# A fused audio-tower kernel: the factors of heads 2 to 7 get a PSUM bank of their own

## The chip, the core and the metric

The kernel runs on one core of one Trainium2 chip. A core has a matrix engine (TensorE, PE in the profile, with its weight loads as PEld), a vector engine (VectorE, DVE), an activation engine (ScalarE, ACT), a general engine (GpSimd, POOL) and queues that issue transfers (SP). Matmuls write to PSUM, which has eight banks of 2 KiB per partition; a 375-column float32 result takes one. The metric is the device time of one launch in microseconds; lower is better.

## What is computed

Sixteen sequences of 750 x 64 pass a token mixer (four 64 x 64 layers, a strided convolution to 375 positions), a retention layer, a product-key memory with attention over it, an inner gradient step of a two-layer network, and a mixture of experts. Nearly all the time is in the product-key memory:

```python
sim = jnp.einsum('pbnhd,pkhd->pbnhk', q, pk_keys)          # two halves, 64 keys each
scores, idx = jax.lax.top_k(sim, 16)                       # of each half
score = scores[0][..., :, None] + scores[1][..., None, :]  # 256 candidates
final_scores, pk_idx = jax.lax.top_k(score, 16)            # 16 of 4096 rows
final_scores = jax.nn.softmax(final_scores, axis=-1)
k = jnp.einsum('bnhk,bnhkd->bnhd', final_scores, keys_table[ind])
v = jnp.einsum('bnhk,bnhkd->bnhd', final_scores, values_table[ind])
```

The kernel doesn't gather the 16 rows. For each head and position it builds the dense row of 4096 weights, which is zero but at the 16 picks, and multiplies it with the whole table of 4096 x 128 (keys and values side by side).

## The kernel before

**Steps and slots.** A sequence has 8 heads, a head has 32 chunks of 128 table rows, so there are 256 steps per sequence. Step j makes the weights of one chunk in a bank of `dense` and sums them into `accu`. The work is spread over slots: in slot j PE runs the `spread` matmul of step j-2 (L506), the `accu` matmul of step j-6 (L520, float32), and the `hot` matmul of step j (L528). ACT reads the bank of step j-2 into `dense_w` (L904, counted by the semaphore `taken`), then applies a steep ramp in place to the bank of step j (L910, `past`). POOL multiplies `dense_w` by the first factor (L449, `weighed`). `hot` of step j may start when its bank is free.

**Factors.** The steps of a head read four factors (k = 0 to 3) that DVE has made in rows (`ranks`, `firsts`, `seconds`). PE turns each by three matmuls into PSUM (k=0 at L492, k=1 in float32 at L494, k=2 and 3 at L496), and ACT copies it into `store` (L890, L892, L894, counted by `factor_kept`). The factors of head 0 come ahead of slot 0, those of head 1 in slots 0, 2, 4 and 6, the 24 of heads 2 to 7 in every second slot from 30 to 76.

**The ring.** Steps and factors take the three banks of `dense` in turn, in the order of `ORDER.items`. So the n-th item waits for the reader of item n-3. Without a factor between, that is step j-3; with one among the last three, it is step j-2, whose `taken` is ACT's work of the same slot.

**What lies between the slots.** Each engine's program is in a fixed, hand-written order. While the slots of sequence b run, the other layers run in between, in pieces: `prepare(b + 1)` (mixer, convolution, layer norm, retention) with `FILL_PREPARE` slots between its pieces (slots 19 to 51), `similarities(b + 1, 0)`, `gradient(b - 1)` with `FILL_GRADIENT` slots between (52 to 81), and later the attention of b. In slots 28 to 82 the pieces on PE are, in order: turning the first norm (L467), the projections (L580, L581), the retention scores (L586, L588), the retention mix (L595), turning the second norm (L467), the similarities (L611), and in the gradient L710, L716, L720, L723, L729 and L736. DVE works on the same chain: the norms (L1147), the rotation (L1197), the decay (L1202), the silu products (L1380 to L1397), and between them it makes the rows of the factors, with a comparison (L1294) and a reduction (L1299) for each pair of heads.

**The two banks `sims`.** The projections and the retention use both; the similarities use both and are copied out by ACT (L956); the gradient uses only the second, `sims[:, 1]`; the attention's scores use both.

## Time and profile before

| | |
|---|---|
| time, median of 3 runs | 6420.99 us (6412.18 to 6425.69) |
| the profiled execution | 6410.07 us, span 6408.2 us |
| PE busy | 5616.6 us, 88% of the span |
| ACT busy | 4644.2 us, 72% |
| DVE busy | 4242.5 us, 66% |
| POOL busy | 4212.2 us, 66% |
| PE's granted clock, mean | 0.974 of full |

The profile shows one execution. A row of a timeline gives start, duration, engine, line and operation, and in brackets the idle time of the engine ahead of it with what ended it. Instructions of one engine overlap in the records (a matmul's record of 0.33 us is followed by the next start 0.16 us later), so the distance between starts tells what an instruction costs, not its duration. The 16 sequences follow each other about 370 us apart. The timelines below are of sequence 5 (the sixth) where nothing else is said.

### The profile page before, as it was taken

To read this page: it belongs to the slowest core of one execution; us is meant where nothing else is said; L and a number is where in the kernel's file an instruction comes from. 1 tells how busy PE (TensorE), PEld (TensorE's weight loads), DVE (VectorE), ACT (ScalarE), POOL (GpSimd) and SP (SyncE) were. 2 spreads that over 40 slices of the span, in tenths; PEclk is the share of its full clock that TensorE was granted. 3 is DMA by queue.
4 is the path that set the end of the run, shared out by engine and by line. 5 is a ranking of instruction groups with operands and counts; after the bars stand their busy time and mean duration, and the time that the engine had idled before them with its cause. 6 is when DMAs were issued, how large, how long until landed. Compare 5 with 4: busy or idle time off the path is not lost.

```text
span 6408.2 us, 79708 instructions
## 1 busy us (share of the span) xinstructions
PE 5616.6 (88%) x24704; PEld 3125.1 (49%) x24704; DVE 4242.5 (66%) x13138; ACT 4644.2 (72%) x10889; POOL 4212.2 (66%) x4108
## 2 busy tenths in 40 slices
PE   2599998989989898989989898899989899999977
PEld 1345454545545454454545455454545545454533
DVE  7676766848585784858568484957758485772157
ACT  1577777878777786877778787777778777777833
POOL 0386766858586685958677585867768585777700
PEclk9999999999999999999999999999999999999968
DMA  1111111111111111111111111111111111111100
GB/s 35 37 56 41 50 48 41 56 37 56 42 50 46 47 52 37 56 39 53 46 47 52 40 53 39 53 46 47 52 37 58 38 53 43 49 48 50 45 21 15
DMA packets 93462, 290.42 MB, mean 45 GB/s; under 512 B 17880, under 2 KB 26547, under 8 KB 92781
## 3 DMA queue, kind: packets, MB, share of 16 engines
q1 hardware_dynamic: 92748, 285.25, 13.5%
q8 instruction: 197, 3.23, 0.2%
q14 instruction: 229, 1.87, 0.1%
q10 hardware_dynamic: 288, 0.07, 0.0%
HBM read 280.68 MB, written 4.61 MB: 45 GB/s over the span
## 4 chain that ended last, share of the span: by engine, by line
PE 60%; POOL 16%; ACT 16%; DVE 6%; issue 2%; DMA 0%; SPq 0%; DVEq 0%; ACTq 0%
PE accu L520 26%; POOL dense_w L449 16%; PE dense L528 9%; PE dense L506 7%; ACT dense L910 4%; ACT dense_w L904 3%; PE sims L641 3%; PE work L647 2%; PE work L568 1%; PE work L685 1%; PE dense L494 1%; PE dense L816 1%; PE work L634 1%; PE work L621 1%; PE sims L611 1%
## 5 line engine op out<-in xcount | busy, mean ns | idle before, releaser
L449 POOL TENSOR_TENSOR dense_w<-dense_w,store 128x375 f32<-128x375 f32 x4096 | 4209.8, 1049 | 1868.2 <-ACT dense_w L904 1825.2
L520 PE MATMUL accu<-dense_w,store 128*128 128x375 f32 x8192 | 3321.8, 488 | 182.4 <-POOL dense_w L449 123.4
L910 ACT ACTIVATE dense<-dense 128x375 f32<-128x375 f32 x4096 | 1917.1, 468 | 782.5 <-PE dense L528 540.1
L904 ACT ACTIVATE dense_w<-dense 128x375 f32<-128x375 f32 x4096 | 1962.4, 479 | 218.1 <-PE dense L506 216.5
L520 PEld LDWEIGHTS accu<-dense_w,store 128*128 128x128 f32 x8192 | 1434.8, 194 | 496.1 <-POOL dense_w L449 172.0
L528 PE MATMUL dense<-store,hot 128*128 128x375 bf16 x4096 | 1337.8, 327 | 250.1 <-ACT dense_w L904 248.6
L506 PE MATMUL dense<-store,spread 96*128 96x375 bf16 x4096 | 1348.5, 329 | 13.7 <-ACT dense L910 11.0
L528 PEld LDWEIGHTS dense<-store,hot 128*128 128x128 bf16 x4096 | 394.8, 97 | 1114.6 <-ACT dense_w L904 703.3
L1299 DVE TENSOR_REDUCE store<-picks 125x256 bf16<-125x4096 uint16 x192 | 848.6, 4420 | 6.6
L506 PEld LDWEIGHTS dense<-store,spread 96*128 96x128 bf16 x4096 | 402.1, 98 | 793.8 <-ACT dense L910 560.2
L1294 DVE TENSOR_TENSOR picks<-codes,keys 125x4096 uint16<-125x4096 uint16 x192 | 527.7, 2749 | 7.3 <-ACTq L897 1.9
L1340 DVE TENSOR_TENSOR shared<-sims,mask 125x750 f32<-125x750 f32 x64 | 59.9, 936 | 407.5 <-PE sims L641 407.5
L1361 DVE TENSOR_TENSOR h<-h_now,work 125x192 f32<-125x192 f32 x16 | 5.7, 354 | 303.7 <-PE work L694 303.7
L647 PE MATMUL work<-shared 125*64 125x375 f32 (+2 forms) x768 | 195.8, 391 | 10.4 <-ACT shared L1010 10.4
L1340 DVE TENSOR_TENSOR prob_odd<-sims,mask 125x750 f32<-125x750 f32 x64 | 59.9, 936 | 198.4 <-PE sims L641 198.4
L641 PE MATMUL sims<-kvT,qT 128*125 128x125 f32 (+2 forms) x768 | 184.7, 376 | 0.2 <-ACT kvT L915 0.2
L1247 DVE TENSOR_TENSOR cand<-s 125x16 f32<-125x16 f32 (+5 forms) x384 | 181.4, 541 | 1.1
L1231 DVE FIND_INDEX8 i<-s,front 125x8 uint32<-125x64 f32 x768 | 165.4, 215 | 0.0
L1232 DVE MATCH_REPLACE8 front<-s,front 125x64 f32<-125x64 f32 x768 | 158.0, 206 | 0.0
L1221 DVE MAX8 s<-front 125x8 f32<-125x64 f32 x768 | 101.9, 210 | 84.5 <-ACT front L956 83.9
L1242 DVE FIND_INDEX8 i<-s,front 125x8 uint32<-125x64 f32 x768 | 150.2, 217 | 0.0
L1380 DVE SCALAR_TENSOR_TENSOR shared<-work,mb_s,shared 64x375 f32<-64x375 f32 x16 | 9.6, 600 | 202.5 <-ACT shared L1036 202.5
(255 smaller groups left out, 6048.1 us busy)
## 6 DMA issues: line engine op xcount, KB each, us to landing
store<-in SPq DMA_DIRECT2D x513, 512.0 KB, 3.3
x_in<-in SPq DMA_DIRECT2D x16, 187.5 KB, 2.4
store<-in SPq DMA_DIRECT2D x1, 2048.0 KB, 8.7
queries_kept<-n3T SPq DMA_DIRECT2D x16, 93.8 KB, 3.4
h_saved<-h SPq DMA_DIRECT2D x16, 93.8 KB
store<-queries_kept SPq DMA_DIRECT2D x16, 93.8 KB, 2.4
store<-h_saved SPq DMA_DIRECT2D x16, 93.8 KB
out<-store SPq DMA_DIRECT2D x16, 93.8 KB
```

Of the source, the lines that this page charges most:

```text
L449: nc.gpsimd.tensor_tensor(dense_w[:, i % RING, :], dense_w[:, i % RING, :], first_of[:, i // CHUNKS, :], ALU.mult).then_inc(s["weighed"], 1)
L506: mm(dense[:, ORDER.step[i] % BANKS, 0:S], spread[0:3 * I1S, c % (CHUNKS // GROUPS), :], second_of[0:3 * I1S, c // (CHUNKS // GROUPS), h, ...
L520: last = mm(accu[:, 0, 0:S], table[:, n % PIECE_RING, i % PIECE, :], dense_w[:, i % RING, :], start=(c == 0), stop=(c == CHUNKS - 1))
L528: mm(to[:, 0:S], hot[:, j % CHUNKS, :], ranksT[:, j // CHUNKS, :], start=True, stop=True, skip_group_check=True).then_inc(s["coded"], 1)
L641: last = mm(dst, qT[:, h % 2, tile(i)], kvT[:, h, 0:(i + 1) * P], start=True, stop=True)
L647: last = mm(work[D:128, 0, j * P:S], vo[:, j, h * D:(h + 1) * D], pT[:, min(j, 1), (0, 0, 2 * P)[j]:(S, 2 * P, S)[j]], start=(h == 0 and j ...
L904: fn(dense_w[:, i % RING, :], dense[:, ORDER.step[i] % BANKS, 0:S], ACT.Relu, scale=-1.0).then_inc(s["taken"], 1)
L910: fn(here, here, ACT.Relu, scale=FAR).then_inc(s["past"], 1)
L1231: v.max_index(i16[:, g, 0:8], s16[:, g, 0:8], rest[:, g, :])
L1247: v.tensor_tensor(cand[:, :, off:off + m], s16[:, H:, 0:m], s16[:, 0:H, a:a + 1].broadcast_to([P, H, m]), ALU.add)
L1294: v.tensor_tensor(hit, codes[:, h:h + 2].unsqueeze(3).broadcast_to([P, 2, 2, SUB, K]), keys[:].unsqueeze(1).unsqueeze(1).broadcast_to([P, ...
L1299: v.tensor_reduce(ranks[:, t, h:h + 2, :].rearrange("p h (a i) -> p h a i", a=2), hit, AX_X, ALU.min).then_inc(s["pick_step"], 1)
```

## The change

The factors of heads 0 and 1 stay in the ring. Those of heads 2 to 7 are written to `sims[:, 0]` and read from there by ACT. Their slots are now 30, 32, 34, 36 (ahead of the projections, which need `sims`), then 46, 48, 50 (after the retention), then every second slot from 52 to 84: none stands any more in slots 38 to 44, and four stand in 78 to 84. A factor waits until ACT has kept the one before it. PE waits for the kept factors (`sims_free`) ahead of the projections and ahead of each of the three similarities. `wait_ge(sim_kept)` after the first similarities now stands for the second sequence too.

```diff
+PREPARE_AT = EARLY
+ROTATE_AT = PREPARE_AT + sum(FILL_PREPARE[:6])
+MIXED_AT = PREPARE_AT + sum(FILL_PREPARE[:8])
+GRADIENT_AT = PREPARE_AT + sum(FILL_PREPARE)
+OWN_BANK = 2
+LATER_SLOTS = [*range(ROTATE_AT - 8, ROTATE_AT, 2), *range(MIXED_AT, GRADIENT_AT, 2)]
+LATER_SLOTS += [GRADIENT_AT + 2 * n for n in range((H - OWN_BANK) * FACTORS - len(LATER_SLOTS))]
...
-            if self.factor_at(j) is not None:
+            if self.factor_at(j) is not None and self.factor_at(j)[0] < OWN_BANK:
                 items.append(("factor", self.factor_at(j)))
...
-                to = bank_free(b, ORDER.factor[h, k])
+                if h < OWN_BANK:
+                    to = bank_free(b, ORDER.factor[h, k])
+                else:
+                    pe.wait_ge(s["factor_kept"], (b * H + h) * FACTORS + k)
+                    to = sims[:, 0]
...
                 pe.wait_ge(s["nT_done"], b * 2 + 1)
+                sims_free(b, ROTATE_AT)
...
+            def sims_free(b, j):
+                if b >= 1:
+                    turned_so_far = OWN_BANK * FACTORS + sum(at < j for at in LATER_SLOTS)
+                    pe.wait_ge(s["factor_kept"], (b - 1) * H * FACTORS + turned_so_far)
+
             def similarities(b, t):
 
+                sims_free(b, GRADIENT_AT if t == 0 else SLOTS)
...
-                n = ORDER.factor[h, k]
                 act.wait_ge(s["factored"], (b * H + h) * FACTORS + k + 1)
-                src = dense[:, n % BANKS, 0:S]
+                src = (dense[:, ORDER.factor[h, k] % BANKS] if h < OWN_BANK else sims[:, 0])[:, 0:S]
```

Three places of PE's order follow, each with before first and the change second. Lines of the changed kernel are 13 to 20 higher (L506 is L519, L520 is L533, L528 is L541, L494 is L507, L496 is L509, L492 is L505).

First place: slots 34 to 35, after the first norm is turned. Before:

```order
L467 MATMUL work<-ident,nrm 64x125 [waits ln_n]
L467 MATMUL work<-ident,nrm 64x125 x2
L506 MATMUL dense<-store,spread 128x375 [waits past]
L496 MATMUL dense<-ident_b,store 96x125 [waits factor_kept]
L496 MATMUL dense<-ident_b,store 96x125 x2
L520 MATMUL accu<-dense_w,store 128x375 [waits weighed]
L528 MATMUL dense<-store,hot 128x375 [waits taken]
```

After:

```order
L476 MATMUL work<-ident,nrm 64x125 [waits ln_n]
L476 MATMUL work<-ident,nrm 64x125 x2
L519 MATMUL dense<-store,spread 128x375 [waits past]
L509 MATMUL sims<-ident_b,store 96x125 [waits factor_kept]
L509 MATMUL sims<-ident_b,store 96x125 x2
L533 MATMUL accu<-dense_w,store 128x375 [waits weighed]
L541 MATMUL dense<-store,hot 128x375 [waits taken]
```

The instructions and their order are the same; the factor writes `sims`, and the `taken` that the last row waits for is that of step 31 now (j-3) and was that of step 32 (j-2).

Second place: slots 38 and 39, after the projections. Before:

```order
L581 MATMUL sims<-halves,wrope_s 64x375
L506 MATMUL dense<-store,spread 128x375 [waits past]
L492 MATMUL dense<-ident_b,store 128x125 [waits factor_kept]
L492 MATMUL dense<-ident_b,store 128x125 x2
L520 MATMUL accu<-dense_w,store 128x375 [waits weighed,acc_done,piece_in0]
L528 MATMUL dense<-store,hot 128x375 [waits taken]
L506 MATMUL dense<-store,spread 128x375 [waits past]
L520 MATMUL accu<-dense_w,store 128x375 [waits weighed]
L528 MATMUL dense<-store,hot 128x375 [waits taken]
```

After:

```order
L595 MATMUL sims<-halves,wrope_s 64x375
L519 MATMUL dense<-store,spread 128x375 [waits past]
L533 MATMUL accu<-dense_w,store 128x375 [waits weighed,acc_done,piece_in0]
L541 MATMUL dense<-store,hot 128x375 [waits taken]
L519 MATMUL dense<-store,spread 128x375 [waits past]
L533 MATMUL accu<-dense_w,store 128x375 [waits weighed]
L541 MATMUL dense<-store,hot 128x375 [waits taken]
```

The factor is gone from here, as from slots 40, 42 and 44.

Third place: slots 77 and 78, after the gradient's last matmuls. Before:

```order
L736 MATMUL work<-dzt,xt 65x64 x5
L506 MATMUL dense<-store,spread 128x375 [waits past]
L520 MATMUL accu<-dense_w,store 128x375 [waits weighed]
L528 MATMUL dense<-store,hot 128x375 [waits taken]
L506 MATMUL dense<-store,spread 128x375 [waits past]
L520 MATMUL accu<-dense_w,store 128x375 [waits weighed,piece_in1]
L528 MATMUL dense<-store,hot 128x375 [waits factor_kept]
```

After:

```order
L756 MATMUL work<-dzt,xt 65x64 x5
L519 MATMUL dense<-store,spread 128x375 [waits past]
L533 MATMUL accu<-dense_w,store 128x375 [waits weighed]
L541 MATMUL dense<-store,hot 128x375 [waits taken]
L519 MATMUL dense<-store,spread 128x375 [waits past]
L505 MATMUL sims<-ident_b,store 128x125 [waits factor_kept]
L505 MATMUL sims<-ident_b,store 128x125 x2
L533 MATMUL accu<-dense_w,store 128x375 [waits weighed,piece_in1]
L541 MATMUL dense<-store,hot 128x375 [waits taken]
```

The first factor of head 7 stands here now; the other three follow in slots 80, 82 and 84.

## Rows read from the trace of the kernel before

**Rows 1.** The page: the group of `hot` matmuls with its idle time.

```profile
L528 PE MATMUL dense<-store,hot 128*128 128x375 bf16 x4096 | 1337.8, 327 | 250.1 <-ACT dense_w L904 248.6
```

**Rows 2.** Windows, `hot` matmuls alone: steps with factors (sequence 15), without.

```profile
5793.12:5815.07 21.95, 5.29 (x16) 1.52 (x17) 1.00 0.16 51
2251.61:2259.23 7.62, 2.57 (x8) 0.77 (x8) 1.00 0.21 67
```

**Rows 3.** Timeline of PE, slots 63 to 65, the first with a float32 factor.

```profile
2161.70 0.83 PE L494 MATMUL dense<-ident,store 125*128 125x125 f32 x6
2162.37 0.80 PE L520 MATMUL accu<-dense_w,store 128*128 128x375 f32 x2
2163.00 0.32 PE L528 MATMUL dense<-store,hot 128*128 128x375 bf16 x1
...
2164.27 0.33 PE L528 MATMUL dense<-store,hot 128*128 128x375 bf16 x1 [0.15 <-ACT dense_w L904]
...
2164.61 0.33 PE L496 MATMUL dense<-ident_b,store 125*96 125x125 bf16 x3
2164.77 0.85 PE L520 MATMUL accu<-dense_w,store 128*128 128x375 f32 x2
```

**Rows 4.** Timeline of ACT in the same slots.

```profile
2163.36 0.47 ACT L910 ACTIVATE dense<-dense 128x375 f32<-128x375 f32 x1 [0.32 <-PE dense L528]
2163.74 0.48 ACT L904 ACTIVATE dense_w<-dense 128x375 f32<-128x375 f32 x1
```

**Rows 5.** Timeline of PE, the pieces between the slots, slots 28 to 77.

```profile
2095.82 1.44 PE L568 MATMUL work<-tapdiag,mixed 128*125 128x64 f32 x11
2106.15 0.48 PE L467 MATMUL work<-ident,nrm 125*64 125x125 f32 x3
2111.74 0.84 PE L580 MATMUL work<-halves,wrope_s 64*64 64x375 f32 x2
2126.44 1.42 PE L595 MATMUL work<-v_s,shared 125*125 125x64 f32 x12
2135.82 0.48 PE L467 MATMUL work<-ident,nrm 125*64 125x125 f32 x3
2150.13 0.84 PE L716 MATMUL work<-x,params 64*64 64x375 f32 x2
2158.21 0.84 PE L720 MATMUL sims<-x,params 64*64 64x375 f32 x2
2168.54 0.84 PE L723 MATMUL work<-halves,w1T_s 64*64 64x375 f32 x2
2182.42 0.75 PE L736 MATMUL work<-dzt,xt 125*65 125x64 f32 x10
```

**Rows 6.** Timeline of DVE: the ends of the chains that PE waits for.

```profile
2102.89 1.32 DVE L1147 TENSOR_SCALAR nrm<-h,mv,rstd 125x64 f32<-125x64 f32 x3
2125.60 0.28 DVE L1202 TENSOR_TENSOR shared<-sims,decay 125x125 f32<-125x125 f32 x1
2159.69 0.60 DVE L1380 SCALAR_TENSOR_TENSOR shared<-sims,mb_s,shared 64x375 f32<-64x375 f32 x1 [0.84 <-ACT shared L1036]
2167.27 1.22 DVE L1397 TENSOR_TENSOR halves<-shared 64x375 f32<-64x375 f32 x1
```

**Rows 7.** Windows, all engines: slots 28 to 76 of sequence 5.

```profile
2097.26:2182.42 85.16, 74.51 (x359) 38.24 (x358) 41.38 (x141) 61.86 (x142) 49.32 (x49) 1.00 0.12 38
```

**Rows 8.** Timeline of POOL while DVE runs L1294 (slots 38 to 41).

```profile
2116.72 5.11 POOL L449 TENSOR_TENSOR dense_w<-dense_w,store 128x375 f32<-128x375 f32 x3 [0.41 <-ACT dense_w L904]
```

**Rows 9.** Timeline of PE after L716, sequences 5 and 6; then a window of 6.

```profile
2154.10 0.33 PE L528 MATMUL dense<-store,hot 128*128 128x375 bf16 x1 [2.00 <-ACT dense_w L904]
...
2526.86 0.33 PE L528 MATMUL dense<-store,hot 128*128 128x375 bf16 x1 [2.01 <-ACT dense_w L904]
...
2532.18 0.84 PE L720 MATMUL sims<-x,params 64*64 64x375 f32 x2
...
2526.00:2532.20 6.20, 5.19 (x17) 2.63 (x17) 5.02 (x5) 4.08 (x10) 4.20 (x4) 0.72 0.00 0
```

More of the change, by code:

```diff
@@ L37 @@
 FACTORS = 4
-PREPARED_EVERY, LATER_FROM = 2, 30
+PREPARED_EVERY = 2
 PIECE = 8
@@ L66 @@
 assert sum(PICKS_INSIDE) == PIECES_SOON
+PREPARE_AT = EARLY
[5 more added lines that the diff above has]
+LATER_SLOTS += [GRADIENT_AT + 2 * n for n in range((H - OWN_BANK) * FACTORS - len(LATER_SLOTS))]
+assert LATER_SLOTS[-1] < GRADIENT_AT + sum(FILL_GRADIENT) + FILL_FIRST[0]
 class Schedule:
@@ L86, in factor_at @@
     def factor_at(j):
-        if j >= LATER_FROM:
-            j -= LATER_FROM - FACTORS * PREPARED_EVERY
-        elif j >= FACTORS * PREPARED_EVERY:
-            return None
-        n, odd = divmod(j, PREPARED_EVERY)
-        n += FACTORS
-        return divmod(n, FACTORS) if odd == 0 and n < H * FACTORS else None
+        if j < FACTORS * PREPARED_EVERY:
+            n, odd = divmod(j, PREPARED_EVERY)
+            return (1, n) if odd == 0 else None
+        if j in LATER_SLOTS:
+            return divmod(OWN_BANK * FACTORS + LATER_SLOTS.index(j), FACTORS)
+        return None
 ORDER = Schedule()
@@ L756, in ahead @@
                 similarities(b, 0)
+                pe.wait_ge(s["sim_kept"], b * NT + 1)
                 if behind:
-                    pe.wait_ge(s["sim_kept"], b * NT + 1)
                     gradient(b - 2, True)
```

## The prediction

> **What bounds the kernel now.** I began with the page. PE is busy 88% of the span, so time is won only where PE stands idle or is kept from its next instruction. The group to look at is the `hot` matmul: PE sat idle 248.6 us before it, all told, until ACT had emptied a bank into `dense_w` [rows 1]. That number counts only recorded idleness; the records overlap, so the real loss is larger, and I took it from distances between starts.
>
> Those distances are in the windows [rows 2]. In sequence 15, where nothing else runs in between, the 16 steps from slot 30 to 45 with eight factors took 21.95 us, or 1.372 us a step. Eight steps without factors took 7.62 us, or 0.953 a step, with PE busy throughout. What should such steps cost with factors? PE's timeline gives the price of a factor in PE's own time [rows 3]: from the first float32 factor matmul to the next `accu` is 2162.37 - 2161.70 = 0.67 us, and for a bf16 factor 2164.77 - 2164.61 = 0.16. Three bf16 factors and one float32 make 1.15 us for four, 0.29 on average. So two steps with one factor need 2 x 0.953 + 0.29 = 2.20 us of PE and take 2 x 1.372 = 2.74. **A factor in the ring costs 0.54 us of stall.**
>
> The next two views show where the stall comes from [rows 3, 4]. `hot` of one slot starts at 2163.00, ACT's ramp for it at 2163.36, ACT's `dense_w` for the step before at 2163.74, which ends at 2164.22, and the next `hot` starts at 2164.27: PE and ACT take turns, in a loop of 1.27 us. The loop exists because the ring makes `hot` of step j wait for step j-2. With only steps in the ring it waits for step j-3, whose copy ACT has made one slot earlier, and the loop is open. ACT itself can follow: its starts are 0.38 us apart [rows 4], so a slot with a factor asks 3 x 0.38 = 1.14 us of it and one without 0.76, together 1.90 for the two slots, under PE's 2.20.
>
> **The change part by part.** Moving the target of the factors costs no instruction; the matmuls, the copies and their kinds are the same. I go through one sequence by the pieces that stand between the slots [rows 5], and ask at each whether the other engines are ready when PE comes earlier [rows 6].
>
> Slots 28 to 33, two factors: the convolution ends at 2097.26, the norm is turned at 2106.15. Twice 0.54 is 1.1 us, and ACT's square root with its table load falls in here, which the ring passes on to PE at once. The norm is ready at 2102.89 + 1.32 = 2104.21, so at most 1.94 can be won. I take 1.5.
>
> Slots 34 to 37, two factors, up to the projections at 2111.74: 2 x 0.54, I take 1.1. The new wait for kept factors ahead of them costs nothing: the last of them is issued in slot 36, ACT copies it ahead of that slot's ramp, and slot 37 lies between.
>
> Slots 38 to 45, from 2111.74 to the retention mix at 2126.44. Here the four factors leave altogether, so PE's part shrinks by 8 x (1.372 - 0.953) = 3.35 us. But the mix waits for DVE, which makes the rows of the last two heads (L1294, L1299) between the rotation and the decay. The decay ends at 2125.60 + 0.28 = 2125.88, only 0.56 ahead of the mix, and it hangs on the projections, not on the slots. I take 0.5; PE now waits some 2.8 us there.
>
> Slots 46 to 51, three factors, up to the second turning at 2135.82: 3 x 0.54 = 1.6. ACT's square root comes after three of these slots and sets DVE's norm, but comes earlier with them. I take 1.4, to leave it something.
>
> Slots 52 to 57 with the similarities ahead, three factors, 2135.82 to 2150.13: 1.6.
>
> Slots 58 to 68, from L716 at 2150.13 to L723 at 2168.54, six factors: 3.2 us by the ring. But L723 starts 0.05 us after DVE's L1397 ends (2167.27 + 1.22 = 2168.49), and in that whole chain DVE had idled only 0.84 us, before the second L1380 [rows 6]. I take 0.8, and PE waits 2.4 us.
>
> Slots 69 to 76, four factors, L723 to L736 at 2182.42: 4 x 0.54 = 2.2. PE also waits here for ACT's copy of `accu` at the change of head, which a faster slot doesn't shorten: 2.0.
>
> Slots 77 to 85: four factors have moved in where PE ran at its full pace, three bf16 and the float32 one: minus 1.2 (the ends are 1.15, PE's own time alone, and 4 x (2.74 - 2 x 0.953) = 3.3, if they stalled as in the ring). I take the first, since no bank of the ring is touched. DVE's wait for the last factor (`factors_out`) is ahead of its next comparison and far behind slot 84.
>
> The sum is 1.5 + 1.1 + 0.5 + 1.4 + 1.6 + 0.8 + 2.0 - 1.2 = **7.7 us per sequence**. The later slots hold no factors and keep their distances, and attention follows PE, so nothing there takes it back. Fourteen sequences (1 to 14) are like this: 108 us. Sequence 0 has no gradient between its slots: 3.1 up to the mix, 1.4, then 13 factors without a DVE chain (7.0) minus 1.2, makes 10.3. Sequence 15 has no `prepare`: 11 factors in slots 28 to 51 at 0.54 plus the four that leave (1.2) is 7.1, then 1.6 + 0.8 + 2.0 - 1.2 = 3.2, also 10.3. In all 108 + 20.6 = 129 us. The profiled span of 6408.2 us becomes 6279; its time of 6410.07 lies 11 us under the median of the three runs, so against the median I say 6421 - 129 = **6292 us**.
>
> **Where POOL stands.** POOL had 49.32 us of work in the 85.16 us of slots 28 to 76 [rows 7]; in 77 to 78 us that is 64%, so it doesn't become the bound on average. While DVE ran L1294 three of its multiplications took 5.11 us, 1.70 each [rows 8], against 49.32 / 49 = 1.01. That happens once in these slots, and PE's new wait for the mix follows it. The Trainium skill (SBUF — State Buffer, "Who interferes with whom") says that only the port pair that DVE and GpSimd share makes engines block each other, and that a DVE operation with two SBUF inputs holds off a reading GpSimd; the trace agrees (1.70 against 1.01 us). By that rule the number of blocked multiplications stays what it is, since DVE's list is unchanged, and the sum is the same.
>
> **The clock.** After PE's wait of 2.01 us in sequence 6 the mean granted clock was 0.72 in a window of 6.2 us, so part of it went at 1.2 GHz and not at 2.4; after the same wait of 2.00 us in sequence 5 it stayed full [rows 9]. From that `hot` to L720 it is 5.32 us in sequence 6 (2526.86 to 2532.18) and 4.11 in sequence 5 (2154.10 to 2158.21, with [rows 5]): such a stretch costs 1.21 us. The change makes two new waits of over 2 us and shortens this one. I count no change in the sum. If each new wait were followed by such a stretch, it would cost 2 x 1.21 us in 14 sequences, 34 us, and the sum would end at 6326; if one in two is, as with the two waits of these rows, at 6309. The Trainium skill (TensorE: Matmul & The Clock Gate, "HAM oscillation — how this bites in real kernels") says that a PE which waits between bursts of matmuls is throttled to half rate and begins the next burst slow, which speaks against this change; by that rule 6326, by the rows' one in two 6309.
>
> **The rivals.** (a) *Nothing on DVE holds PE.* Then all 24 factors give 0.54: 13 us in each of 16 sequences, 207 us, 6214. Against it stand the 0.56, 0.05 and 0.84 us [rows 5, 6]; for it, that DVE's own operations could move forward too. (b) *Half is given back*, by the clock as above and by ACT, whose copies and table loads between the slots then come due at the same moment as PE: 3 to 4 us a sequence less, about 6350. (c) *It doesn't do what it says*: the steps with factors are slow for ACT's sake, not the ring's, and stay at 1.37. Against it: the loop of 1.27 also appears in a slot without a factor copy [rows 3, 4]. About 6421. (d) *Slower*: the waits for the mix and for L723 leave PE at half clock for the slots between them. A step at PE's own pace would then cost another 0.95 us, so the change loses from eight such steps a sequence on (7.7 / 0.95); with twelve it would be 6421 + 16 x 3.7 = 6480. For it is only that the clock did fall after 2.01 us; against it, that in sequence 6 it cost no more than 1.21.
>
> **How the numbers follow.** Forecast (6260 to 6325): 0.62. (a) 0.09. (b) 0.20. (c) 0.05. (d) 0.04. The range from 6238 to 6355 holds the forecast, the near part of (a) and most of (b). A difference of 0.2%, 13 us, is about what the runs can tell from none. Faster: 0.62 + 0.09 + 0.20 = 0.91; same 0.05; slower 0.04.
>
> **What the profile after would show.** Right: the 16 steps of sequence 15 in some 17.6 us and not 21.95; the idle time before `hot` for ACT down to well under 100 us; PE waiting for DVE before the mix (some 2 to 3 us) and before L723 (2 to 2.5 us); slots 77 to 85 longer by 1.2 us. Wrong: no such waits and a distance of over 10 us won per sequence is (a); windows at a clock below 1.00 in slots 42 to 69 of most sequences are (b) or (d); steps still at 1.3 us are (c).

## The result and the profile after

| | before | after |
|---|---|---|
| time, median of 4 runs | 6417.88 us | 6373.84 us (6368.5 to 6375.23) |
| ratio | | 0.9924 [0.9912, 0.9936] |
| the profiled execution, span | 6408.2 us | 6371.0 us |
| PE's granted clock, mean | 0.974 | 0.966 |

The change makes the kernel faster: the medians are 44 us apart (0.7%), and the ratio of the table says 0.76%. I had said 129 us and a range that ended at 6355, so the sign was right and the size was not.

The page of the changed kernel first, with the `hot` group that answers to [rows 1] and the `accu` group beside it.

```profile
L541 PE MATMUL dense<-store,hot 128*128 128x375 bf16 x4096 | 1337.1, 327 | 159.3 <-ACT dense_w L923 157.8
...
L533 PE MATMUL accu<-dense_w,store 128*128 128x375 f32 x8192 | 3336.4, 490 | 197.9 <-POOL dense_w L458 135.6
```

PE's recorded idle time before `hot`, counted where ACT's `dense_w` ended it, fell from 248.6 to 157.8 us. I had expected well under 100.

The window of `hot` alone in sequence 15, slots 30 to 45 (it answers to the first of [rows 2]), and three slots of its timeline on PE, one with a bf16 factor and one without.

```profile
5765.76:5784.09 18.33, 5.16 (x17) 1.54 (x16) 1.00 0.18 58
```

```profile
5770.27 0.33 PE L509 MATMUL sims<-ident_b,store 125*96 125x125 bf16 x3
5770.44 0.85 PE L533 MATMUL accu<-dense_w,store 128*128 128x375 f32 x2
5771.12 0.32 PE L541 MATMUL dense<-store,hot 128*128 128x375 bf16 x1
...
5772.08 0.32 PE L541 MATMUL dense<-store,hot 128*128 128x375 bf16 x1
```

The loop of two slots is open: a step without a factor takes 5772.08 - 5771.12 = 0.96 us beside a factor, where [rows 3] had 1.27, and `hot` starts without a wait. So the bank does what it was meant to do. To find where the gain went, I took from both traces the distance between the starts of `hot` for twelve stretches of the 256 slots, averaged over sequences 1 to 14. The table holds those that differ in one of the kernels below; slots 8 to 28 take 36.2 us and slots 190 to 255 take 90.3 in all. Each line is one profiled execution. It can lie off the median of its kernel ("before" 8 us under it, "before, rows late" 15 over, "packed in the wait" 13 over). Of the 20 us between the first two, kernels of equal median, slots 4 to 8 and 98 to 190 hold 13.

| slots | 4–8 | 28–38 | 38–46 | 46–52 | 52–62 | 62–69 | 69–77 | 77–86 | 86–98 | 98–190 |
|---|---|---|---|---|---|---|---|---|---|---|
| before | 9.86 | 17.54 | 13.29 | 12.95 | 19.70 | 10.13 | 13.81 | 9.75 | 11.93 | 107.97 |
| **after** | 10.79 | 15.26 | 14.03 | 12.48 | 16.81 | 10.23 | 12.36 | 11.08 | 13.80 | 108.38 |
| slots only | 9.90 | 17.31 | 13.54 | 13.30 | 20.05 | 10.14 | 13.80 | 12.73 | 12.47 | 107.58 |
| rows late | 10.94 | 15.26 | 10.75 | 11.48 | 16.95 | 10.23 | 12.08 | 11.08 | 13.81 | 108.10 |
| before, rows late | 10.54 | 17.54 | 13.29 | 12.91 | 19.99 | 10.14 | 13.81 | 9.75 | 11.93 | 108.22 |
| packed | 8.59 | 15.26 | 14.39 | 12.27 | 19.42 | 9.98 | 11.41 | 9.74 | 11.94 | 108.11 |
| both | 9.64 | 15.25 | 10.75 | 11.39 | 19.51 | 9.97 | 11.41 | 9.74 | 11.92 | 107.93 |
| kept busy | 11.12 | 15.25 | 13.10 | 12.20 | 16.98 | 10.23 | 12.08 | 11.08 | 13.80 | 108.37 |
| no comparison | 11.35 | 15.25 | 13.84 | 12.48 | 16.77 | 10.23 | 12.68 | 11.08 | 11.95 | 106.93 |
| before, none | 9.93 | 17.54 | 13.29 | 12.64 | 19.96 | 10.13 | 13.80 | 9.76 | 11.48 | 108.44 |
| early, rows late | 10.71 | 17.42 | 10.75 | 12.14 | 17.05 | 10.26 | 12.13 | 9.74 | 11.92 | 108.40 |
| early | 9.54 | 17.42 | 13.61 | 12.00 | 16.98 | 10.29 | 12.42 | 9.74 | 11.92 | 108.13 |
| earlier, rows late | 10.38 | 17.43 | 10.75 | 12.83 | 16.33 | 10.16 | 11.17 | 9.74 | 11.93 | 107.98 |
| packed in the wait | 9.56 | 15.26 | 10.75 | 11.57 | 17.14 | 10.81 | 12.08 | 9.74 | 11.93 | 108.36 |

Read the first two lines. In slots 28 to 77 the change wins 6.25 us a sequence, where my terms said 8.9. Then it loses 1.33 in slots 77 to 86 (I said 1.2), 1.87 in 86 to 98, 0.93 in 4 to 8 and 0.41 in 98 to 190 (I said nothing for all three). That leaves 1.7 us a sequence. Fourteen of them make 24 us, sequence 0 won 6.9 and sequence 15 won 7.7: 39 us in all, against a span that is 37.2 us shorter.

The same in one sequence: PE's pieces between the slots of sequence 5 in the changed kernel, which answer to [rows 5].

```profile
2085.78 1.44 PE L581 MATMUL work<-tapdiag,mixed 128*125 128x64 f32 x11
...
2094.94 0.51 PE L476 MATMUL work<-ident,nrm 125*64 125x125 f32 x3 [0.41 <-DVE nrm L1166]
...
2099.64 0.84 PE L594 MATMUL work<-halves,wrope_s 64*64 64x375 f32 x2
...
2113.82 1.52 PE L609 MATMUL work<-v_s,shared 125*125 125x64 f32 x12 [2.08 <-DVE shared L1221]
...
2123.96 0.51 PE L476 MATMUL work<-ident,nrm 125*64 125x125 f32 x3
...
2137.24 0.84 PE L736 MATMUL work<-x,params 64*64 64x375 f32 x2
...
2154.60 0.84 PE L743 MATMUL work<-halves,w1T_s 64*64 64x375 f32 x2 [1.48 <-DVE halves L1416]
...
2166.75 0.87 PE L756 MATMUL work<-dzt,xt 125*65 125x64 f32 x12
```

From the projections (L594) to the mix (L609) it is 14.18 us and was 14.70; from the mix to the second turning (L476) 10.14, and was 9.38. PE's wait of 2.08 us for the decay (L1221) was forecast. The loss behind it was not. PE's wait for DVE before L743, 1.48 us, is shorter than the 2 to 2.5 that I had said.

### The profile page after: what moved, and what is told of

Read it like the earlier page. It is cut to its first block, busy times and chain, and to the rows that moved or that the text cites. A ratio compares the mean times of both kernels' runs of the same rounds, so it can differ in the third digit from the quotient of the medians.

```text
span 6371.0 us, 79739 instructions
## 1 busy us (share of the span) xinstructions
PE 5590.7 (88%) x24704; PEld 3177.0 (50%) x24704; DVE 4253.6 (67%) x13138; ACT 4624.6 (73%) x10889; POOL 4211.8 (66%) x4108
## 3 DMA queue, kind: packets, MB, share of 16 engines
q14 instruction: 228, 1.87, 0.1%
## 4 chain that ended last, share of the span: by engine, by line
PE 60%; POOL 15%; ACT 11%; DVE 11%; issue 2%; DMA 0%; SPq 0%; DVEq 0%; ACTq 0%
PE accu L533 28%; POOL dense_w L458 15%; PE dense L541 7%; PE dense L519 7%; PE sims L661 3%; PE work L667 2%; ACT dense L929 2%; DVE store L1318 2%; PE work L581 1%; ACT dense_w L923 1%; PE work L705 1%; PE dense L836 1%; DVE nrm L1166 1%; PE work L654 1%; DVE picks L1313 1%
## 5 line engine op out<-in xcount | busy, mean ns | idle before, releaser
L533 PE MATMUL accu<-dense_w,store 128*128 128x375 f32 x8192 | 3336.4, 490 | 197.9 <-POOL dense_w L458 135.6
L533 PEld LDWEIGHTS accu<-dense_w,store 128*128 128x128 f32 x8192 | 1438.8, 194 | 510.6 <-issue 167.1
L541 PE MATMUL dense<-store,hot 128*128 128x375 bf16 x4096 | 1337.1, 327 | 159.3 <-ACT dense_w L923 157.8
L519 PE MATMUL dense<-store,spread 96*128 96x375 bf16 x4096 | 1352.1, 330 | 20.8 <-ACT dense L929 16.9
L519 PEld LDWEIGHTS dense<-store,spread 96*128 96x128 bf16 x4096 | 402.8, 98 | 918.9 <-ACT dense L929 605.4
L541 PEld LDWEIGHTS dense<-store,hot 128*128 128x128 bf16 x4096 | 396.8, 97 | 772.5 <-ACT dense_w L923 266.0
L1266 DVE TENSOR_TENSOR cand<-s 125x16 f32<-125x16 f32 (+5 forms) x384 | 157.8, 479 | 1.1
L667 PEld LDWEIGHTS work<-shared 125*64 125x64 f32 x768 | 100.4, 144 | 97.3 <-issue 66.5
```

Of the source, the lines that this page charges most:

```text
L519: mm(dense[:, ORDER.step[i] % BANKS, 0:S], spread[0:3 * I1S, c % (CHUNKS // GROUPS), :], second_of[0:3 * I1S, c // (CHUNKS // GROUPS), h, ...
L533: last = mm(accu[:, 0, 0:S], table[:, n % PIECE_RING, i % PIECE, :], dense_w[:, i % RING, :], start=(c == 0), stop=(c == CHUNKS - 1))
L541: mm(to[:, 0:S], hot[:, j % CHUNKS, :], ranksT[:, j // CHUNKS, :], start=True, stop=True, skip_group_check=True).then_inc(s["coded"], 1)
L667: last = mm(work[D:128, 0, j * P:S], vo[:, j, h * D:(h + 1) * D], pT[:, min(j, 1), (0, 0, 2 * P)[j]:(S, 2 * P, S)[j]], start=(h == 0 and j ...
L1266: v.tensor_tensor(cand[:, :, off:off + m], s16[:, H:, 0:m], s16[:, 0:H, a:a + 1].broadcast_to([P, H, m]), ALU.add)
```

## The experiments

The name of each stands in the table above. All are edits of the changed kernel but the two that say "before", which are edits of the kernel before. Each ratio is against runs of the kernel before that were taken beside the experiment. Their medians were 6417.88 us for the changed kernel, 6414.01 for the first four experiments, 6409.63 for the next four, 6414.92 for the three lists and 6419.98 for the last one, so a distance from one experiment to another of another group, or to the changed kernel, can be off by some 10 us.

### The slots alone

All factors stay in the ring, but in the new slots:

```diff
-            if self.factor_at(j) is not None and self.factor_at(j)[0] < OWN_BANK:
+            if self.factor_at(j) is not None:
...
-                if h < OWN_BANK: ... else: ... to = sims[:, 0]
+                to = bank_free(b, ORDER.factor[h, k])
...
-                src = (dense[:, ORDER.factor[h, k] % BANKS] if h < OWN_BANK else sims[:, 0])[:, 0:S]
+                src = dense[:, ORDER.factor[h, k] % BANKS, 0:S]
```

> The change's slots, but all factors in the ring of three banks. Theory (the bank opens the loop, the slots alone win nothing): steps 30 to 46 of sequence 15 at about 1.37 us again where a factor stands in every second slot, and the whole at the time of before, 6418, within 15 us. Rival (it is the slots that help, since four factors leave slots 38 to 44): near the changed kernel, 6374.

Measured: 6468.79 us, ratio 1.0086 [1.0072, 1.01]. The slots cost 55 us, and so the bank alone is worth 6468.79 - 6373.84 = 95 us. In the table the new slots win next to nothing at slots 38 to 46 (13.54 against 13.29), since PE waits there for DVE in any case, and slots 77 to 86 take 2.98 us more. The direction is my theory's; the number is outside its bounds. The four late factors cost 2.98 us in the ring and 1.33 in the bank of their own. Those are nearly the two ends that the prediction had for them (3.3 and 1.15), and I had left the upper one out of this expectation. PE's wait of 2.08 us before the mix stands in this kernel too, in sequences 1 to 14.

### The rows of the last heads made late

Ahead of the mix, PE waits for the decay, and DVE makes the rows of the last two heads before it. Two rows of DVE in the changed kernel, sequence 5, show it:

```profile
2108.25 4.42 DVE L1318 TENSOR_REDUCE store<-picks 125x256 bf16<-125x4096 uint16 x1
...
2113.49 0.28 DVE L1221 TENSOR_TENSOR shared<-sims,decay 125x125 f32<-125x125 f32 x1
```

The decay ends at 2113.77 and the mix starts at 2113.82. The edit moves what is left of the row making behind the second norm:

```diff
-                for _ in picking:
-                    pass
                 dve.wait_ge(s["ret_mm"], b + 1)
...
                 normalise(h1, ...)
+                for _ in picking:
+                    pass
```

> The changed kernel with DVE's last pair of ranks (one L1294 and one L1299, 7.4 us) moved behind the second layer norm of prepare, where DVE had idled. Theory (PE waits for DVE ahead of the mix, and its clock falls there): slots 38 to 52 shorter by 4 to 5 us in each of 15 sequences, no half clock at slots 45 to 47, in all 6374 - 60 = about 6315. Rival (the clock and other waits take it back, or DVE is late in the gradient instead): less than 20 us under 6374.

Measured: 6305.03 us, ratio 0.9835 [0.9821, 0.9848], 69 us under the changed kernel. The windows of all engines for slots 38 to 45 and 46 to 51 in sequence 5, first of the changed kernel (columns: length, busy time and count of PE, PEld, DVE, ACT and POOL, PE's clock, DMA share, GB/s):

```profile
2103.10:2116.63 13.53, 11.45 (x61) 6.97 (x59) 11.61 (x15) 7.83 (x19) 10.58 (x9) 0.97 0.12 39
2116.63:2129.18 12.55, 10.24 (x48) 5.77 (x46) 3.73 (x15) 8.40 (x20) 5.05 (x6) 0.90 0.01 1
```

and of this experiment:

```profile
2080.84:2091.59 10.75, 10.75 (x60) 6.97 (x59) 3.87 (x10) 7.54 (x19) 8.22 (x9) 1.00 0.11 32
2091.59:2103.70 12.11, 9.79 (x47) 5.53 (x46) 8.77 (x10) 9.05 (x21) 8.27 (x7) 0.93 0.04 17
```

PE is busy for all of the 10.75 us, and DVE has 3.87 us of work there where it had 11.61. The wait for the mix is gone in every sequence, and with it the half clock in slots 44 to 47. So the wait and what followed it held back 69 us (65 when each kernel is set against its own runs of the kernel before), where the change had won 44.

### The same edit on the kernel before

> The same move in the kernel before. Theory (before the change the ring, not DVE, sets the pace ahead of the mix; DVE ends 0.56 us ahead of it): 6418 within 15 us. Rival (the rows of DVE also held up the old kernel): over 20 us faster.

Measured: 6414.71 against 6414.01 us, ratio 1.0 [0.9991, 1.0009]; slots 38 to 46 stay at 13.29. Before the change PE's wait there costs nothing, although the decay ended only 0.56 us ahead of the mix: with the factors in the ring, the slots themselves fill the time. This is the cleanest reading of the study. The eight slots took 13.29 us with four factors in the ring and 14.03 with the wait for DVE in their place. It is the move of the factors that brings the wait out: "slots only" has it as well, and 13.54 us. The 0.5 us between the two go with the half clock, which follows the wait in 3 sequences there and in 13 after the change.

### The late factors packed into the gradient

No factor stands behind slot 74; from 58 to 68 there is one in every slot:

```diff
-LATER_SLOTS += [GRADIENT_AT + 2 * n for n in range((H - OWN_BANK) * FACTORS - len(LATER_SLOTS))]
+LATER_SLOTS += [*range(GRADIENT_AT, 58, 2), *range(58, 69), 70, 72, 74]
```

> The changed kernel with the late factors in slots 52, 54, 56, 58 to 68 (each slot), 70, 72, 74, none from 76 on. Theory (PE waits 2 us for DVE before the gradient's dx anyway, and after slot 77 it runs at its full pace): 1.2 us less in slots 77 to 85, and POOL's blocked multiplications fall later against PE, so up to 1.9 us less in 86 to 98; 15 x 2 to 3 us, about 6335. Rival (a single bank can't take a factor a slot, PE waits for ACT): 6374 or slower.

Measured: 6318.87 us, ratio 0.9856 [0.9841, 0.9871], 55 us under the changed kernel. Slots 77 to 86 are back at 9.74 and 86 to 98 at 11.94, so both losses come from the four late factors, though none stands behind slot 84. Slots 52 to 62 lose 2.61, slots 69 to 77 win 0.95. I had expected some 39 us. The larger part of the 55, 2.20 us in each of 14 sequences or 31 us, stands in slots 4 to 8, which no edit touches (see the section on the prediction), so the 55 are not the price of the late factors alone; 1.34 + 1.86 us a sequence, 45 us, is what the table gives for them, against 20 lost in slots 52 to 77.

### Both edits

> The changed kernel with both moves: DVE's last ranks behind the second norm, and the late factors packed into slots 52 to 74. Theory (the two waits are apart, in slots 38 to 52 and 77 to 98): the gains over 6374 add up, 69 + 55, so about 6250. Rival (both take from the same clock stretches at slots 4 to 7, or DVE's ranks, now later, meet the packed factors): 6290 or more.

Measured: 6263.23 us, ratio 0.9761 [0.9748, 0.9775]. The two gains, 69 and 55 us, would make 6250; 111 of the 124 us arrive. Slots 52 to 62 still take 19.51. The rows of ACT and PE in sequence 5 show why:

```profile
2104.53 1.28 ACT L1052 ACT_TABLE_LOAD   x1
...
2107.75 0.46 ACT L914 CAST store<-sims 96x375 bf16<-96x375 f32 x1
```

```profile
2108.26 0.37 PE L510 MATMUL sims<-ident_b,store 125*96 125x125 bf16 x3 [2.03 <-ACT store L914]
```

With one bank for the factors, the factor of slot 59 waits for ACT's copy of that of slot 58, and ACT comes to it behind a table load and three operations of the gradient. Without a factor in slot 59 ("early, rows late" below) slots 52 to 62 are back at 17.05 us.

### PE kept busy in the wait

If the half clock behind the wait costs something by itself, it should go when PE has matmuls to do in the wait. Their results are not used:

```diff
+                for _ in range(12):
+                    mm(sims[:, 1, 0:S], hot[:, 0, :], ranksT[:, 0, :], start=True, stop=True)
                 pe.wait_ge(s["ret_done"], b + 1)
```

> The changed kernel with twelve idle matmuls (375 columns, bf16, results unused) in PE's wait ahead of the mix. Theory (what the wait costs beyond itself is the half clock that follows at slots 45 to 47): 38 to 46 stays at 14 us or 0.9 less, 46 to 52 loses 1 us or so, no half clock at 45 to 47, in all 15 to 30 us under 6374. Rival (the clock falls there for the window's sake, whatever PE does, or its cost is hidden behind ACT's square root): 6374 within 10.

Measured: 6351.01 us, ratio 0.9897 [0.988, 0.9915], 23 us under the changed kernel though PE does more. Against their own runs of the kernel before the two are 15 us apart, and their intervals just touch (0.9915 and 0.9912), so by time alone the gain is small and uncertain. The table is clearer: slots 38 to 46 take 13.10 instead of 14.03. No half clock stands in slots 44 to 47 any more, but in 11 sequences it does in 48 to 51, so 0.93 + 0.28 us a sequence, 17 us, is a lower bound for what the clock takes there.

### Without the comparison of the first tile

In slots 86 to 98 the changed kernel loses 1.87 us. The rows of DVE, POOL and PE there, sequence 5:

```profile
2180.27 2.86 DVE L1293 TENSOR_TENSOR picks<-pos,runs 125x2048 f32<-125x2048 uint32 x1
...
2187.82 2.75 DVE L1313 TENSOR_TENSOR picks<-codes,keys 125x4096 uint16<-125x4096 uint16 x1
```

```profile
2180.13 11.28 POOL L458 TENSOR_TENSOR dense_w<-dense_w,store 128x375 f32<-128x375 f32 x8 [1.58 <-ACT dense_w L923]
```

```profile
2184.02 0.90 PE L533 MATMUL accu<-dense_w,store 128*128 128x375 f32 x2 [0.35 <-POOL dense_w L458]
...
2191.46 0.90 PE L533 MATMUL accu<-dense_w,store 128*128 128x375 f32 x2 [1.45 <-POOL dense_w L458]
```

While DVE runs each of the two, one multiplication of POOL takes 3.0 us, and PE then waits 0.35 and 1.45 us for POOL. To see whether that is the loss, the edit leaves out, for the first tile of positions and in sequences 1 to 15, the comparison that assigns the picks to their runs; a reduction over one input stands in its place, so the picks of that tile are not the reference's.

```diff
-                v.tensor_tensor(over_k, pos[:]..., runs[:]..., ALU.is_ge)
+                if t == 0 and b >= 1:
+                    v.tensor_reduce(over[:, :, 0:K], over_k, AX_X, ALU.add)
+                else:
+                    v.tensor_tensor(over_k, pos[:]..., runs[:]..., ALU.is_ge)
```

> The changed kernel, where the comparison over_k of position tile 0 (two inputs in SBUF, 2.9 us, while a POOL multiplication takes 3.0) is left out in sequences 1 to 15 and a reduction of the same tile (2.3 us) runs in its place; so the picks of tile 0 are not the reference's. Theory (POOL, held twice within 7.4 us, is late for accu in slots 86 to 98): these slots take about 12 us and not 13.8, so 14 x 1.5 to 1.9, some 25 us under 6374. Rival (the 1.9 us there are ACT's, which waits for DVE's exponent differences): 6374 within 10.

Measured: 6332.73 us, ratio 0.9872 [0.9857, 0.9888], 41 us under the changed kernel where I had expected some 25 (33 against their own runs of the kernel before). The window of slots 86 to 97 in the changed kernel:

```profile
2179.34:2193.15 13.81, 12.01 (x49) 6.26 (x48) 13.57 (x16) 10.56 (x26) 13.02 (x11) 1.00 0.17 61
```

and in this experiment:

```profile
2164.11:2176.07 11.96, 11.75 (x50) 6.40 (x49) 11.72 (x16) 11.03 (x26) 11.08 (x11) 1.00 0.21 68
```

POOL does the same eleven pieces in 1.94 us less, and the stretch is 1.85 us shorter. Another 1.45 us a sequence comes in slots 98 to 190, and 1.0 of it goes with PE's clock: in slots 98 to 104 it is at half in 3 of sequences 1 to 14, in the changed kernel in 13. Sequences at full clock there take 106.76 against 107.16 us. So 26 us, in slots 86 to 98, is what this experiment shows of the comparison.

### The same on the kernel before

> The same omission in the kernel before (picks of tile 0 not the reference's). Theory (there the second hold falls under ACT's own stop at slot 98, so holds cost only 0.46 us): 6418 within 12 us, at most 8 faster. Rival (the hold costs the same everywhere): 25 us faster.

Measured: 6401.32 us, ratio 0.9982 [0.9972, 0.9992]; slots 86 to 98 go from 11.93 to 11.48. In these slots the comparison costs 0.45 us a sequence before the change and 1.85 after it; in the whole it is 8 us before and 33 to 41 after, clock and all. DVE's instruction is the same. In the kernel before, the two holds fell three steps later, on steps 88 and 94, and the second lay under a stop that ACT made anyway. This is PE's row at that stop, in the kernel before:

```profile
2209.10 0.33 PE L528 MATMUL dense<-store,hot 128*128 128x375 bf16 x1 [2.27 <-ACT dense_w L904]
```

### Three lists with the factors ahead of the similarities

"Early, rows late" fills slots 30 to 37, one a slot, and ends at 76; "early" is the same without the late rows; "earlier" fills 46 to 51 too and ends at 70.

```diff
+LATER_SLOTS = [*range(30, 38), 46, 48, 50, *range(52, 77, 2)]
...
+LATER_SLOTS = [*range(30, 38), *range(46, 52), *range(52, 71, 2)]
```

> DVE's last ranks behind the second norm, and the factors of heads 2 and 3 in slots 30 to 37 (each slot), the others in 46, 48, 50 and every second slot from 52 to 76: none after 76 and none in a slot next to one in the gradient. Theory (what the packed slots lost in slots 52 to 62, 2.6 us a sequence, is PE's factor in slot 59 waiting for ACT to keep the one of slot 58): 52 to 62 back at 17 us, 77 to 98 at 21.7 as with the packed slots, 28 to 38 at most 1 us longer; about 6263 - 14 x 1.6 = 6240. Rival (a factor in each of slots 30 to 37 keeps PE waiting for ACT by as much): 6263 or slower.

Measured: 6296.53 us, ratio 0.9809 [0.9796, 0.9822]. Slots 77 to 98 are back at 21.66 together, but slots 28 to 38 take 17.42, 2.2 more. This is the rival's case: a factor in every slot loses what the bank had won. The theory's own part held: without a factor in slot 59, slots 52 to 62 take 17.05.

> The same slots with DVE's last ranks where the change has them. Theory (the wait ahead of the mix is worth 60 to 69 us on its own, whatever the slots): 6240 + 65 = about 6305. Rival (with the early factors PE comes to the mix later and waits less): within 30 us of the run with both.

Measured: 6327.52 us, ratio 0.9858 [0.9843, 0.9873]. The late rows are worth 31 us here and 69 in the changed kernel. Slots 38 to 46 take 13.61 instead of 10.75, 2.9 us a sequence, which by itself is 40 us; 1.2 us come back in slots 4 to 8, where no edit stands. PE waits 2.08 us before the mix here too, but its clock falls behind it in 5 sequences and not in 13, and slots 46 to 52 win nothing (12.00 against 12.14) where they won 1.0 from the changed kernel. 31 us is neither my 65 nor within the rival's 30: I had overrated how far the worth of this edit can be carried over.

> DVE's last ranks behind the second norm, factors in slots 30 to 37 and 46 to 51 (each slot) and every second slot from 52 to 70. Theory (ACT's share, 1.14 us in a slot with a factor against PE's 1.12, is the bound in packed slots, and slots 46 to 51 have little room ahead of the norm): 46 to 52 longer by 1 us, 69 to 77 shorter by 1, the same as the run with slots to 76 within 15 us. Rival (the more is done early, the better): over 15 us faster.

Measured: 6278.07 us, ratio 0.9776 [0.9759, 0.9792], 18 us under the first of the three and so just past my 15. The gain stands in slots 69 to 77 (11.17 against 12.13) and 52 to 62 (16.33 against 17.05), less 0.7 in slots 46 to 52.

### Packed where PE waits anyway

Before L743 PE waits for DVE's chain. Factors in every slot from 62 to 70 should lie in that wait, and leave slots 30 to 60 as they were:

```diff
+LATER_SLOTS = [30, 32, 34, 36, 46, 48, 50, *range(52, 62, 2), *range(62, 71), 72, 74, 76]
```

with the late rows as well.

> DVE's last ranks behind the second norm; factors in every second slot from 30 to 36 and 46 to 60, in each slot from 62 to 70, then in 72, 74 and 76. Theory (a factor next to a factor costs where PE has no wait to hide it, slots 28 to 38 and 58 to 62, and nothing in slots 62 to 69, where PE waits for DVE): 28 to 38 at 15.3 us, 52 to 62 at 17, 62 to 69 at 10 to 10.3, 77 to 98 at 21.7; 14 x 2.2 us under the run with both moves (6263), so about 6235. Rival (each slot costs ACT the same everywhere, or PE's clock takes it back): 6255 or more.

Measured: 6248.93 us (6236.27 to 6277.5), ratio 0.9738 [0.9715, 0.9761]. It is the fastest version of the study, 2.6% under the kernel before, though its interval overlaps that of "both", and it is half of the 28 us that I had expected under it. The windows of slots 38 to 45, 52 to 61 and 62 to 68, 77 to 85 and 86 to 97 in sequence 5:

```profile
2064.83:2075.58 10.75, 10.75 (x61) 6.97 (x60) 3.87 (x10) 7.54 (x19) 8.23 (x9) 1.00 0.12 31
...
2086.88:2103.65 16.77, 15.33 (x71) 7.66 (x70) 8.51 (x23) 14.10 (x33) 10.05 (x10) 1.00 0.15 44
2103.65:2114.46 10.81, 10.74 (x58) 5.91 (x57) 10.67 (x66) 8.97 (x23) 7.85 (x9) 1.00 0.08 31
...
2126.54:2136.28 9.74, 9.74 (x41) 5.11 (x40) 9.64 (x64) 8.06 (x19) 8.16 (x9) 1.00 0.26 80
2136.28:2148.21 11.93, 11.72 (x49) 6.39 (x48) 11.65 (x46) 10.56 (x26) 11.14 (x11) 1.00 0.19 69
```

The stretch that took the packed factors is longer than in the changed kernel (10.81 against 10.23, more than the 10 to 10.3 expected), and PE is busy for 10.74 us of it. What is left in slots 62 to 98 is nearly all PE's own work.

## Why the prediction was wrong

**What held.** The steps with factors were slow for the ring's sake (rival (c) is out): the bank is worth 95 us by the first experiment, in the new slots. PE waits 2.08 us for DVE before the mix (I said 2 to 3) and slots 77 to 86 lose 1.33 us (I said 1.2). From the projections to the mix the gain is 0.52 us in sequence 5 (I said 0.5). In the others the terms were a little large. The measured gains in sequence 5 are 1.2 us from the convolution to the first turning (I said 1.5), 0.9 up to the projections (1.1), 1.0 from the second turning to L736 (1.6), 1.05 from there to L743 (0.8) and 1.7 up to L756 (2.0). Four of the five are 0.2 to 0.6 us under. One reason is the 0.54 itself (below). Rivals (a) and (d) are out: DVE does hold PE, and the kernel is faster.

**The step that failed first: "Slots 46 to 51 ... I take 1.4."** Measured in sequence 5: minus 0.8; on average of sequences 1 to 14 the stretch from the mix to the second turning went from 9.38 to 10.48 us, minus 1.1, which is 2.5 short of the term and by far the largest miss of one. The mechanism stands in PE's rows behind the mix:

```profile
2115.51 1.32 PE L533 MATMUL accu<-dense_w,store 128*128 128x375 f32 x2
...
2116.63 0.52 PE L541 MATMUL dense<-store,hot 128*128 128x375 bf16 x1
...
2117.26 1.46 PE L533 MATMUL accu<-dense_w,store 128*128 128x375 f32 x2
...
2118.51 0.52 PE L541 MATMUL dense<-store,hot 128*128 128x375 bf16 x1
```

A `hot` record of 0.52 us and not 0.32 is the mark of the lower level, 1.2 GHz. The step takes 2118.51 - 2116.63 = 1.88 us, and the granted clock of slots 46 to 51 is 0.90. ACT's square root comes three of these slots later, and the norm behind it gates the second turning:

```profile
2121.20 0.29 ACT L887 ACTIVATE std<-mv,eps 125x3 f32<-125x3 f32 x1
...
2121.51 0.17 DVE L1163 RECIPROCAL rstd<-std 125x3 f32<-125x3 f32 x1 [4.92 <-ACT std L887]
...
2121.73 2.17 DVE L1166 TENSOR_SCALAR nrm<-h,mv,rstd 125x64 f32<-125x64 f32 x3
```

DVE had idled 4.92 us for that square root. In sequence 3 the clock stayed at full behind the mix. There the second turning comes 8.46 us after the mix; in nine sequences with a short stretch at half clock it comes after 10.1, and in four with a longer one after 11.8. That prices the half clock behind the mix within one execution, 9 x 1.67 + 4 x 3.31 = 28 us. Sequence 3 won 0.92 us and not 1.4, and the last row shows what held it back: the third of DVE's three scalings runs beside a multiplication of POOL and takes 1.01 us where it took 0.30 before the change, 0.7 us on the way to the turning. The first norm pays the same 0.7, and PE waits 0.41 us for it ahead of the first turning; that stretch won 1.2 and not 1.5.

**"I count no change in the sum"** for the clock. I counted, by the granted clock, where the half clock stands. In slots 44 to 47 it is 13 sequences, of the 14 in which PE waits for the decay (sequence 0 has no such wait and keeps its clock), and none before the change, when it was 8 sequences in slots 48 to 51; that is 2 now. In slots 4 to 7 it is 14 sequences, and was 7. In slots 98 to 104 it is 13 of sequences 1 to 14, and was 7. The stretches of slots 56 to 59, in 8 sequences before, are gone. With those of slots 51 to 53 they made 2.55 us in each of seven sequences, 18 us, which the change got back; so the clock's balance in slots 46 to 62 is smaller than the 28 us. I had priced a stretch at 1.21 us, once per new wait at most, and taken none; behind the mix it measured 1.67 and 3.31. The Trainium skill (TensorE: Matmul & The Clock Gate, "HAM oscillation — how this bites in real kernels") says, of a kernel whose waits are longer than these, that a PE that waits between bursts begins the next one slow. This trace agrees, with 13 of 14 after a wait of 2.08 us. But the wait alone does not decide it: with the same 2.08 us in the same 14 sequences the clock fell in 14 of them in "packed" and "no comparison", in 5 in "early" and in 3 in "slots only"; without the wait it fell there in no kernel. What else it takes is open. Rival (b) named this mechanism, with half of the gain as its price.

The window of slots 4 to 7 of sequence 5 in the changed kernel:

```profile
2039.92:2051.63 11.71, 10.67 (x33) 5.98 (x33) 1.05 (x4) 6.09 (x18) 3.64 (x4) 0.56 0.00 0
```

and in the kernel before:

```profile
2053.65:2061.67 8.02, 6.67 (x33) 3.66 (x33) 1.04 (x4) 6.07 (x18) 3.66 (x4) 1.00 0.00 0
```

The same 33 instructions take 3.7 us more, at half clock. The kernel before has both values too: 8.02 us in the seven odd sequences up to 13, 11.71 in the seven even ones from 2 to 14. After the change 11.71 stands in eight of the fourteen, and 8.02 in one. No edit of this change stands near these slots, and the table has them anywhere from 8.59 to 11.35 in fourteen executions. What decides it I have not found; 0.93 us a sequence, 13 us of the shortfall, stays open, and with it what makes the clock fall in slots 98 to 104, where the 0.41 us of slots 98 to 190 stand.

**"The later slots hold no factors and keep their distances"** failed for slots 86 to 98: 1.87 us a sequence, 26 us in all. DVE's two comparisons now hold POOL three steps earlier (steps 85 and 91, not 88 and 94), where ACT has no stop of its own to hide it. Four factors shift PE's slots by 1.33 us against DVE's list. The other 2.0 us come from DVE, whose list is fixed in its order and not in its time: from slot 77 to the first comparison it was 14.0 us and is 12.0. In between stand eight short additions with two inputs in SBUF, first before and then after the change:

```profile
2186.76 4.26 DVE L1247 TENSOR_TENSOR cand<-s 125x128 f32<-125x128 f32 x8
...
2171.10 2.16 DVE L1266 TENSOR_TENSOR cand<-s 125x128 f32<-125x128 f32 x8
```

Before, POOL multiplied all through them, and every second one had to wait: the fourth took 0.99 us. Now POOL pauses in their middle, 0.69 us for ACT, and six of the eight run free of it: the fourth takes 0.18. With no factor behind slot 74 ("packed") the 14.0 us are back, and both comparisons are back on steps 88 and 94. "No comparison" gave the 1.85 us back and its twin on the kernel before 0.45, so the cause of the loss is shown. My own sentence was that "the number of blocked multiplications stays what it is ... and the sum is the same": the number of DVE's operations did stay, the price of a hold did not. The rows show 3.0 us for one multiplication, not 1.70, and it is the place that decides. The Trainium skill (SBUF — State Buffer, "Who interferes with whom") says that a DVE instruction with two SBUF inputs contends with a GpSimd instruction that reads SBUF, that the port pair they share is an exclusive lock, and that the order of issue decides who blocks. The trace agrees in both orders: POOL's multiplication, started 0.67 us behind DVE's comparison of 2.86 us, took 3.03, and DVE's fourth addition, started behind a multiplication, took 0.99 and not 0.18.

**The 17.6 us for sequence 15** was mis-sized by my own working: I counted the ring's eight factors in slots 30 to 45, where the new slots put four. It measured 18.33. In the kernel before, 13 of the 16 steps take 1.27 to 1.29 us, with a factor or without, and the three others 1.63, 2.03 (at the change of head, from slot 37 to 38) and 1.63. I had put the excess of these three, 1.45 us, into the stall of the eight factors. Two steps of 1.28 against the 2.20 of PE's own work make 0.36 us for a factor, not 0.54. The terms whose stretch has no wait for DVE in it agree: 0.34 us a factor from the second turning to L736 in sequence 5, and 0.43 from L743 to L756.

**The sum.** Of the 90 us missing, 6.0 us a sequence make 84 in sequences 1 to 14: 2.6 in slots 28 to 77 (the stretch from the mix to the second turning alone is 2.5 short), 0.1 in 77 to 86, 1.9 in 86 to 98, 0.9 in 4 to 8 and 0.4 in 98 to 190. The rest is in sequences 0 and 15, 3.4 and 2.6 us short of 10.3.

**The bound that I had seen and not used.** I noted that the decay ended only 0.56 us ahead of the mix, and priced that term at 0.5. What I did not ask is what the wait is worth if the work ahead of it moves. The answer is 65 to 69 us, more than the change itself.

## What to carry to other kernels

When a stall is taken away, the wait behind it sets the time, and an edit to that wait, worth nothing before (6414.71 against 6414.01 us), can then be worth more than the change (69 us). Look for it on the engine that finishes last ahead of the new wait, and move what nobody needs yet behind it. A change that shifts one engine against another's fixed list moves the places where they collide, far behind its last edited slot: check the slots behind it, not only those edited. And a list that is fixed in its order is not fixed in time: what the other engine does beside it changes what its operations take.

## What the runs showed of the hardware that was not expected

- One multiplication of POOL over 128 x 375 takes 3.03 us when it starts 0.67 us behind a two-input operation of DVE of 2.86 us: DVE's remaining 2.19 us, and 0.84 of its own. The nine others of slots 86 to 97 in that sequence take 0.84 to 1.03 us each. The hold goes the other way as well: an addition of DVE that takes 0.18 us alone took 0.99 behind a multiplication of POOL, so the same eight took 4.26 us before the change and 2.16 after.
- The third of DVE's three scalings behind the square root took 1.01 us beside a multiplication of POOL, 0.30 without one, and the three together 2.17 against 1.46 us. The Trainium skill's section on who interferes with whom (SBUF — State Buffer, "Who interferes with whom") lists this kind of operation as one that can contend; the trace agrees.
- PE fell to 1.2 GHz behind a wait of 2.08 us in 13 of 14 sequences, and in two other kernels with the same wait in 3 and 5 of 14. With twelve unused matmuls in the wait it stayed at 2.4 GHz in slots 44 to 47 in all of them, fell in slots 48 to 51 in 11, and the kernel was 15 to 23 us faster.
